# Windowed attention: strips masked by small matmuls, plain maxima, products over two or three query tiles, projections over 512 columns

## The chip, the cores and the metric

The kernel runs on one core of one Trainium2 chip. The metric is the device time of one launch in microseconds; lower is better. Engines are PE (TensorE), DVE (VectorE), ACT (ScalarE), POOL (GpSimd) and SP (the queue that issues most transfers). PSUM has eight banks of 128 x 512 fp32.

## The reference

Three layers act on x of shape (4, 2048, 256): a mixture-of-experts layer, an attention layer and the experts again. For the drawn inputs every expert is over its capacity, so that the expert layers add nothing except that their routing must be counted. The attention is what takes the time:

```
q = (x @ Wq.T).reshape(B, T, H, HD); k, v alike        # x here is layer-normed; H = 16 heads, HD = 16
attend = |i - j| <= 128  or  i == 0  or  j == 0
logits = where(attend, q @ k.T * 0.25, -inf)
out = softmax(logits) @ v;  x = x + out @ Wo.T
```

So each query looks at 257 neighbours and at key 0, and query 0 looks at all keys.

## The kernel before

A batch has 16 tiles of 128 tokens; the 16 heads go in four head groups of four. One *item* is one tile of one head group (256 items in all), one *step* handles one item in each stage, and a step has four *quarters*, one for each head. The function `schedule` writes out one global order of events, quarter by quarter, and each engine runs the events that concern it in that order. The stages lag behind one another: A at step k, B at step k - 20, the products with the values (PV) at step k - 23.

- **A (L934, L1431)**: the logits of a query tile for one head, as four strips. Strip s holds 32 queries on partitions 32s to 32s + 31, against a window of 288 keys; each strip is one bf16 matmul (q and k are stacked in bf16 pieces, 96 rows) in a column tile of its own, so that the four run side by side. The bank is one of a ring of three (`a_ring`). Then DVE adds the mask (`band`, fp32 in SBUF, one of three versions: first tile, middle, last tile) and takes the row maximum in one fused instruction (`tensor_tensor_reduce`), followed by a read of the accumulator into `row_max`. Its semaphore `a_free` gives the bank back.
- **MAX**: once per head group the maxima are turned and put as extra rows beside q.
- **B (L962, L1105)**: the logits transposed (keys on partitions), less the maxima, in a ring of two banks (`b_ring`); ACT takes the exponential into `probs`, a ring of four tiles in fp32.
- **CUT (L1218, L1223)**: POOL zeroes the two outer blocks of `probs` outside the band.
- **PV (L980)**: for query tile i, one event for each key tile j = i - 1, i, i + 1, at quarters 0, 1 and 2; each event is four fp32 matmuls (one for each head, each in its own column tile) with the 32 columns of the values as weights and 128 columns of `probs` moving. An fp32 matmul shows as two instructions. Four query tiles share the bank `o_bank`, which COPY_OUT (L1122) then copies for the division.
- **QK (L823)**: the projection of q and k for 512 tokens, fp32, as four events (two halves of 256 columns, two halves k of the contraction), each of four column tiles. ACT, DVE and POOL then cut the result in bf16 pieces and SP stacks them by DMA.
- Further fillers in the order: VALUES (L838), PROJECT (L806), transposes, norms and the work for query 0 (FIRST). `QK_AT`, `VALUES_AT` and the like give the quarter at which each starts, set by hand.

For a wait, `band_count(n)` and `pv_count(n, part)` give how many CUTs and PV events must have been done. The exponential of item n at its first head waits until PV item n - 3 has done the part with key tile n - 4, since `probs` is a ring of four. The constants are loaded by SP at the start (L668, L675).

## Time and profile before

| | us |
|---|---|
| median of 3 runs | 869.26 (867.83 to 869.36) |
| span of the profiled execution | 867.2 |
| PE busy | 814.6 (94%) |
| DVE busy | 758.3 (87%) |
| ACT busy | 637.2 (73%) |
| POOL busy | 488.1 (56%) |

The page gives the span of the profiled execution, from its first to its last instruction; its own device time beside that is not given, and the median of the timed runs lies 2.1 us above the span. How to read it: busy time is a share of the whole span, and a busy PE counts each matmul to the modelled end of its pipeline, so that small holes between matmuls don't show. PE and PEld (weight load) overlap. A distance between two starts says more on what an instruction occupies than its length, since the next one often starts before the end.

### The profile page before, as it was taken

To read this page: it belongs to the slowest core of one execution; us is meant where nothing else is said; L and a number is where in the kernel's file an instruction comes from. 1 tells how busy PE (TensorE), PEld (TensorE's weight loads), DVE (VectorE), ACT (ScalarE), POOL (GpSimd) and SP (SyncE) were. 2 spreads that over 40 slices of the span, in tenths; PEclk is the share of its full clock that TensorE was granted. 3 is DMA by queue.
4 is the path that set the end of the run, shared out by engine and by line. 5 is a ranking of instruction groups with operands and counts; after the bars stand their busy time and mean duration, and the time that the engine had idled before them with its cause. 6 is when DMAs were issued, how large, how long until landed. Compare 5 with 4: busy or idle time off the path is not lost. (4 is left out here: it accounts for less than half of the span.)

```text
span 867.2 us, 50607 instructions
## 1 busy us (share of the span) xinstructions
PE 814.6 (94%) x21504; PEld 606.9 (70%) x21505; DVE 758.3 (87%) x2819; ACT 637.2 (73%) x1417; POOL 488.1 (56%) x874
## 2 busy tenths in 40 slices
PE   9798999999999999999999999898999999999894
PEld 8555667767777777667778777666778777766572
DVE  7898899989887899998987899998988889998785
ACT  2268888897877667998877666898777766888850
POOL 3212556675555557765554465675554556656763
PEclk9999999999999999999999999999999999999998
DMA  7722224432212344441213335352222335220113
GB/s 231 116 81 75 67 73 121 135 88 70 77 62 96 111 146 119 120 127 62 89 51 101 106 105 161 108 131 71 74 73 68 106 93 149 94 77 18 49 51 102
DMA packets 93191, 83.51 MB, mean 96 GB/s; under 512 B 17568, under 2 KB 92192, under 8 KB 92960
## 3 DMA queue, kind: packets, MB, share of 16 engines
q1 hardware_dynamic: 91360, 78.91, 30.1%
q8 instruction: 171, 2.80, 1.5%
q10 hardware_dynamic: 1600, 1.31, 1.0%
q14 instruction: 60, 0.49, 0.2%
HBM read 20.66 MB, written 8.39 MB: 33 GB/s over the span
## 5 line engine op out<-in xcount | busy, mean ns | idle before, releaser
L1105 ACT ACTIVATE probs<-bank 128x384 f32<-128x384 f32 (+1 forms) x1024 | 462.8, 480 | 146.8 <-PE bank L962 137.4
L1431 DVE CUSTOM_DVE_ANT_0 bank<-bank,con 128x288 f32<-128x288 f32 x1024 | 494.4, 518 | 53.2 <-PE bank L934 44.8
L934 PE MATMUL bank<-k_stack,q_stack 96*32 96x288 bf16 x4096 | 325.4, 288 | 10.7 <-DVE row_max L1431 5.7
L962 PE MATMUL bank<-q_stack,k_stack 99*32 99x288 bf16 (+2 forms) x4096 | 319.8, 285 | 16.0 <-ACT probs L1105 9.7
L980 PE MATMUL bank<-probs,v_sb 128*32 128x128 f32 x5888 | 305.4, 272 | 3.6 <-issue 1.5
L1218 POOL TENSOR_SCALAR_AFFINE_SELECT probs<-probs 128x512 f32<-128x512 f32 x240 | 154.8, 645 | 180.1 <-ACT probs L1105 179.5
L980 PEld LDWEIGHTS bank<-probs,v_sb 128*32 128x32 f32 x5888 | 192.1, 110 | 36.7 <-issue 5.3
L962 PEld LDWEIGHTS bank<-q_stack,k_stack 99*32 99x32 bf16 x4096 | 123.6, 95 | 79.7 <-ACT probs L1105 53.5
L934 PEld LDWEIGHTS bank<-k_stack,q_stack 96*32 96x32 bf16 x4096 | 127.3, 95 | 74.0 <-DVE row_max L1431 21.3
L1223 POOL TENSOR_SCALAR_AFFINE_SELECT probs<-probs 128x512 f32<-128x512 f32 x240 | 154.1, 642 | 19.3 <-ACT probs L1105 19.2
L823 PE MATMUL bank<-xnT,wqk_sb 128*32 128x256 f32 x2048 | 158.1, 379 | 0.6 <-DVE neg_max L1453 0.5
L1431 DVE DVE_READ_ACCUMULATOR2_ANT row_max<- 128x1 f32 x1024 | 144.1, 141 | 0.0
L1206 POOL TENSOR_TENSOR pieces<-rest,pieces 128x512 bf16<-128x512 f32 x64 | 74.4, 1162 | 61.7 <-ACT pieces L1070 61.5
L838 PE MATMUL bank<-wv_sb,xnT 128*32 128x272 f32 x1024 | 83.9, 393 | 1.7 <-ACT v_sb L1077 1.1
L806 PE MATMUL bank<-wo_sb,attnT 128*32 128x264 f32 x1024 | 72.0, 386 | 1.9 <-DVE x_ring L1339 0.9
L823 PEld LDWEIGHTS bank<-xnT,wqk_sb 128*32 128x32 f32 x2048 | 64.6, 110 | 5.6 <-ACT v_sb L1077 1.2
L1055 ACT ACTIVATE pieces<-bank 128x512 bf16<-128x512 f32 x64 | 38.3, 599 | 20.7 <-PE bank L823 19.5
L1359 DVE TENSOR_TENSOR rest<-bank,pieces 128x512 f32<-128x512 f32 x64 | 44.1, 688 | 4.3 <-ACT pieces L1055 4.1
L1266 DVE BATCH_NORM_STATS2 stats<-x_ring 128x6 f32<-128x256 f32 x112 | 47.1, 421 | 0.2
L1000 PE MATMUL bank<-con,o_raw 128*32 128x68 f32 x2048 | 44.4, 223 | 2.6 <-issue 1.7
L1070 ACT ACTIVATE pieces<-rest 128x512 bf16<-128x512 f32 x64 | 40.6, 635 | 8.0 <-DVE rest L1359 7.8
L806 PEld LDWEIGHTS bank<-wo_sb,attnT 128*32 128x32 f32 x1024 | 33.2, 109 | 13.4 <-issue 2.2
(126 smaller groups left out, 737.2 us busy)
## 6 DMA issues: line engine op xcount, KB each, us to landing
q_stack<-pieces SPq DMA_DIRECT2D x384, 64.0 KB, 2.7
k_stack<-pieces SPq DMA_DIRECT2D x364, 64.0 KB, 2.7
x_ring<-in_x SPq DMA_DIRECT2D x28, 512.0 KB, 4.5
out_x<-x_ring SPq DMA_DIRECT2D x16, 512.0 KB, 3.9
attn<-in_x SPq DMA_DIRECT2D x4, 512.0 KB, 6.0
wback_sb<-in_wback SPq DMA_DIRECT2D x8, 256.0 KB, 6.0
k_stack<-pieces ACTq DMA_DIRECT2D x20, 64.0 KB, 3.6
q_stack<-neg_max SPq DMA_DIRECT2D x48, 16.0 KB, 2.3
```

What stands on the lines that cost most here:

```text
L806: last = pe.matmul(bank_of("PROJECT", i, t)[SP * s:SP * (s + 1), 0:D + E], attnT[:, t // 2, k, at:at + SP], wo_sb[:, k, :], start=(k == 0) ...
L823: last = pe.matmul(bank_of("QK", g, c)[SP * s:SP * (s + 1), 256 * half:256 * (half + 1)], wqk_sb[:, g % NG, k, SP * s:SP * (s + 1)], xnT[: ...
L838: last = pe.matmul(bank_of("VALUES", b, t)[SP * s:SP * (s + 1), 0:D + HD], xnT[:, k, at:at + SP], wv_sb[:, k, :], start=(k == 0), stop=(k ...
L934: last = pe.matmul(a_ring[i % len(a_ring)][SP * s:SP * (s + 1), 0:WIN], q_stack[g % 2][0:KROWS, h, q:q + SP], k_stack[g % 2][0:KROWS, h, q ...
L962: last = pe.matmul(b_ring[i % len(b_ring)][SP * s:SP * (s + 1), start:final], k_stack[g % 2][0:SROWS, h, WINDOW + P * j + SP * s:WINDOW + ...
L980: last = pe.matmul(o_bank[SP * h:SP * (h + 1), P * (i % 4):P * (i % 4 + 1)], v_sb[:, j, VW * head:VW * head + SP], probs[:, j % 4, h, P * ...
L1105: act.activation(probs[:, j % 4, h, c0:c1], b_ring[i % len(b_ring)][:, c0:c1], ACT.Exp, scale=LOGIT_SCALE).then_inc(S["exp_ready"], 1)
L1206: pool.tensor_tensor(pieces[i % 2][:, 2, :], rest[:, :], pieces[i % 2][:, 1, :], ALU.subtract).then_inc(S["piece3_ready"], 1)
L1218: pool.affine_select(out=part, in_=part, compare_op=ALU.is_ge, fill=0.0, base=0, pattern=[[0, HG], [1, P]], channel_multiplier=-1).then_in ...
L1223: pool.affine_select(out=part, in_=part, compare_op=ALU.is_ge, fill=0.0, base=0, pattern=[[0, HG], [-1, P]], channel_multiplier=1).then_in ...
L1266: dve.bn_stats(stats[:, t, :], x_tiles(i)[:, t, :]).then_inc(S["stats_ready"], 1)
L1431: dve.tensor_tensor_reduce(out=a_ring[i % len(a_ring)][:, 0:WIN], in0=a_ring[i % len(a_ring)][:, 0:WIN], in1=mask, scale=1.0, scalar=con[: ...
```

## The change

Three edits are made together.

1. **Mask.** The masks `band` and the identity are copied to bf16 (`band_half`, `ident_half`) by ACT at the start. After the four matmuls of an A item, PE adds the mask to the strips by matmuls with a piece of the identity as weights: for a middle tile the first 32 and the last 32 columns of the strip (64 columns, one set of four), for the first and last tile of a batch 128 columns on the open side and 32 on the other (two sets). DVE's fused instruction becomes a plain maximum over the 288 columns.
2. **Products.** A PV event is now one key tile against all the query tiles of the same bank that it serves: `products_of(i)` lists (key tile, first query tile, end), two or three tiles wide, or one where a neighbour lies in another bank. `PRODUCTS_AT` sets the quarter: (0, 1), (1), (1), (0, 2) for i mod 4. The waits on counts of PV events follow it.
3. **Projections.** A QK event takes 512 columns in place of 256, so there are two in place of four, at the first and third of the former places.

```diff
@@ -77,6 +77,8 @@
         ones = sb("ones", [P, P])
+        ident_half = sb("ident_half", [P, P], BF16)
+        band_half = sb("band_half", [P, 3, WIN], BF16)
         neg_half = sb("neg_half", [P, 4])
...
@@ -119,7 +121,7 @@
         take = ident.rearrange("p (h c) -> p h c", c=SP)[:, :, 0:VW]
-        band = [con[:, C_BAND + i * WIN:C_BAND + (i + 1) * WIN] for i in range(3)]
+        band_all = con[:, C_BAND:C_BAND + 3 * WIN].rearrange("p (i c) -> p i c", i=3)
         pick = con[:, C_PICK:C_PICK + NG * SP].rearrange("p (g c) -> p g c", g=NG)
...
@@ -361,10 +363,66 @@
+        def products_of(i):
+            parts = []
+            if i % 4 == 0 and i:
+                parts.append((i - 1, i, i + 1))
+            parts.append((i, i - (i % 4 > 0), i + 1 + (i % 4 < 3)))
+            if i % 4 == 3 and i < NT - 1:
+                parts.append((i + 1, i, i + 1))
+            return parts
+        PRODUCTS_AT = ((0, 1), (1,), (1,), (0, 2))
+        pv_before = [sum(len(products_of(t)) for t in range(i)) for i in range(NT + 1)]
         def pv_count(n, part):
             g, i = divmod(n, NT)
-            return g * (3 * NT - 2) + min(3 * i + part, 3 * NT - 2)
+            return g * pv_before[NT] + pv_before[i] + part
+        def pv_last(n):
+            j = n % NT
+            if j % 4 == 3 and j < NT - 1:
+                return pv_count(n + 1, 1)
+            return pv_count(n, 1 + (j % 4 == 0 and j > 0))
+        def mask_of(t):
+            return 0 if t == 0 else 2 if t == NT - 1 else 1
+        def both_edges(strip):
+            return strip.rearrange("p (b c) -> p b c", c=SP)[:, 0:2 * WINDOW // SP + 1:2 * WINDOW // SP, :]
+        def lower_half(strip):
+            return strip[:, 0:WINDOW]
+        def lower_edge(strip):
+            return strip[:, 0:SP]
+        def upper_half(strip):
+            return strip[:, WIN - WINDOW:WIN]
+        def upper_edge(strip):
+            return strip[:, WIN - SP:WIN]
+        def mask_parts(t):
+            if t == 0:
+                return lower_half, upper_edge
+            if t == NT - 1:
+                return lower_edge, upper_half
+            return both_edges,
...
@@ -453,8 +511,8 @@
                         apart = apart if n else OPENING["QK_APART"]
-                    for part in range(4):
-                        begin(at + apart * part, "QK", n, c, part)
+                    for k in range(KC):
+                        begin(at + 2 * apart * k, "QK", n, c, k)
                     done = at + 3 * apart + 1
...
@@ -530,10 +588,12 @@
                         events.append(("A", k, h))
-                    if 0 <= pv < items and h < 3:
-                        if 0 <= pv % NT + h - 1 < NT:
-                            events.append(("PV", pv, h))
-                        if h == 2 and pv % 4 == 3:
+                    if 0 <= pv < items:
+                        i = pv % NT
+                        for part, slot in enumerate(PRODUCTS_AT[i % 4][-len(products_of(i)):]):
+                            if slot == h:
+                                events.append(("PV", pv, part))
+                        if h == 2 and i % 4 == 3:
                             events.append(("COPY_OUT", pv // 4))
...
@@ -668,8 +728,8 @@
                         sp.dma_start(x_tiles(1), rows(dram, 1)).then_inc(S["x_first1"], 16)
+                        sp.dma_start(con[:, C_BAND:C_PICK], consts[:, C_BAND:C_PICK]).then_inc(S["band_in"], 16)
                         for dst, src in (
-                                (con[:, C_BAND:C_PICK], consts[:, C_BAND:C_PICK]),
                                 (con[:, C_DIAG:], consts[:, C_DIAG:]),
...
@@ -809,9 +869,8 @@
                         elif kind == "QK":
-                            g, c, part = n
-                            half, k = divmod(part, KC)
-                            if part == 0:
+                            g, c, k = n
+                            if k == 0:
                                 if g == 0 and first:
...
@@ -819,18 +878,17 @@
                             for s in range(4):
-                                at = 512 * c + 256 * half
-                                last = pe.matmul(bank_of("QK", g, c)[SP * s:SP * (s + 1), 256 * half:256 * (half + 1)],
+                                last = pe.matmul(bank_of("QK", g, c)[SP * s:SP * (s + 1), :],
                                                  wqk_sb[:, g % NG, k, SP * s:SP * (s + 1)],
-                                                 xnT[:, k, at:at + 256],
+                                                 xnT[:, k, 512 * c:512 * (c + 1)],
                                                  start=(k == 0), stop=(k == KC - 1))
-                            if part == 3:
+                            if k == KC - 1:
                                 last.then_inc(full_sem("QK", g, c), 1)
                         elif kind == "VALUES":
                             b, t, k = n
                             if k == 0:
                                 if first and b == 0 and t == 0:
-                                    pe.wait_ge(S["setup_in"], 16 * 5)
+                                    pe.wait_ge(S["setup_in"], 16 * 4)
                                 pe.wait_ge(*emptied("XT", early_index[b, t // 4], t % 4 // 2))
...
@@ -931,10 +990,16 @@
                                 q = P * t + SP * s
-                                last = pe.matmul(a_ring[i % len(a_ring)][SP * s:SP * (s + 1), 0:WIN],
-                                                 q_stack[g % 2][0:KROWS, h, q:q + SP],
-                                                 k_stack[g % 2][0:KROWS, h, q:q + WIN],
-                                                 start=True, stop=True)
+                                pe.matmul(a_ring[i % len(a_ring)][SP * s:SP * (s + 1), 0:WIN],
+                                          q_stack[g % 2][0:KROWS, h, q:q + SP],
+                                          k_stack[g % 2][0:KROWS, h, q:q + WIN],
+                                          start=True, stop=False)
+                            for parts in mask_parts(t):
+                                for s in range(4):
+                                    strip = a_ring[i % len(a_ring)][SP * s:SP * (s + 1), 0:WIN]
+                                    last = pe.matmul(parts(strip), ident_half[:, SP * s:SP * (s + 1)],
+                                                     parts(band_half[:, mask_of(t), :]),
+                                                     start=False, stop=parts is mask_parts(t)[-1])
                             last.then_inc(S["a_full"], 1)
...
@@ -968,20 +1033,20 @@
                             g, i = divmod(n, NT)
-                            j = i - 1 + part
-                            if g % NG == 0 and part == 2 or n % (NG * NT) == 0 and part == 1:
+                            j, first_tile, end_tile = products_of(i)[part]
+                            if g % NG == 0:
                                 pe.wait_ge(*emptied("VALUES", g // NG, j))
                             pe.wait_ge(S["band_ready"], band_count(NT * g + j))
-                            start, final = part == 0 or i == 0 and part == 1, part == 2 or j == NT - 1
-                            if start and n % 4 == 0 and n:
+                            start = i % 4 == 0 and part == 0
+                            if start and n:
                                 pe.wait_ge(S["o_copied"], n // 4)
                             for h in range(HG):
                                 head = HG * (g % NG) + h
                                 last = pe.matmul(
-                                    o_bank[SP * h:SP * (h + 1), P * (i % 4):P * (i % 4 + 1)],
+                                    o_bank[SP * h:SP * (h + 1), P * (first_tile - i // 4 * 4):P * (end_tile - i // 4 * 4)],
                                     v_sb[:, j, VW * head:VW * head + SP],
-                                    probs[:, j % 4, h, P * (i - j + 1):P * (i - j + 2)],
-                                    start=start, stop=final)
+                                    probs[:, j % 4, h, P * (first_tile - j + 1):P * (end_tile - j + 1)],
+                                    start=start, stop=True, skip_group_check=True)
                             last.then_inc(S["pv_done"], 1)
...
@@ -1007,6 +1072,10 @@
                         act.activation(warm[:, :], neg_half[:, 0:1], ACT.Identity)
+                        act.wait_ge(S["ident_in"], 16)
+                        act.activation(ident_half[:, :], ident, ACT.Copy).then_inc(S["masks_ready"], 1)
+                        act.wait_ge(S["band_in"], 16)
+                        act.activation(band_half[:, :, :], band_all, ACT.Copy).then_inc(S["masks_ready"], 1)
                         act.wait_ge(S["pads_ready"], 1)
...
@@ -1099,7 +1168,7 @@
                             if n >= 4 and h == 0:
-                                act.wait_ge(S["pv_done"], pv_count(n - 3, 0))
+                                act.wait_ge(S["pv_done"], pv_last(n - 4))
                             i = HG * n + h
...
@@ -1116,7 +1185,7 @@
                             n, = n
-                            act.wait_ge(S["pv_done"], pv_count(4 * n + 3, 2))
+                            act.wait_ge(S["pv_done"], pv_count(4 * n + 4, 0))
                             if n:
...
@@ -1420,18 +1489,12 @@
                             g, t = divmod(n, NT)
-                            mask = band[0 if t == 0 else 2 if t == NT - 1 else 1]
                             i = HG * n + h
-                            if first and n == 0 and h == 0:
-                                dve.wait_ge(S["setup_in"], 16 * 5)
                             if h == 0 and t == 0 and g >= 2:
                                 dve.wait_ge(S["p0_diff"], g - 1)
                             dve.wait_ge(S["a_full"], i + 1)
-
-                            dve.tensor_tensor_reduce(
-                                out=a_ring[i % len(a_ring)][:, 0:WIN], in0=a_ring[i % len(a_ring)][:, 0:WIN], in1=mask,
-                                scale=1.0, scalar=con[:, C_LOWEST:C_LOWEST + 1], op0=ALU.add,
-                                op1=ALU.max, accum_out=row_max[:, g % 2, h, t:t + 1]).then_inc(S["a_free"], 1)
+                            dve.tensor_reduce(row_max[:, g % 2, h, t:t + 1], a_ring[i % len(a_ring)][:, 0:WIN],
+                                              AX.X, ALU.max).then_inc(S["a_free"], 1)
                         elif kind == "MAX":
                             g, = n
                             if g:
```

## Rows read from the trace of the kernel before

**Rows 1.** The page: span, busy time of each engine, granted clock in 40 slices.

```profile
span 867.2 us, 50607 instructions
PE 814.6 (94%) x21504; PEld 606.9 (70%) x21505; DVE 758.3 (87%) x2819; ACT 637.2 (73%) x1417; POOL 488.1 (56%) x874
...
PEclk9999999999999999999999999999999999999998
```

**Rows 2.** Busy time by engine (with instruction counts), sums over three sets of stretches.

```profile
core 0: us, PE busy (x) PEld busy (x) DVE busy (x) ACT busy (x) POOL busy (x), PEclk, DMA share, GB/s
...
sum 300.00, PE 298.63 PEld 231.73 DVE 254.65 ACT 217.06 POOL 162.17; mean PE 99.55 PEld 77.24 DVE 84.88 ACT 72.35 POOL 54.06
...
sum 273.00, PE 256.18 PEld 182.65 DVE 259.84 ACT 209.61 POOL 157.10; mean PE 51.24 PEld 36.53 DVE 51.97 ACT 41.92 POOL 31.42
...
sum 200.00, PE 185.45 PEld 138.04 DVE 174.69 ACT 171.40 POOL 120.22; mean PE 37.09 PEld 27.61 DVE 34.94 ACT 34.28 POOL 24.04
```

**Rows 3.** Timeline of PE, 238 to 240 us (start, length of the merged run, instructions).

```profile
238.20 0.62 PE L823 MATMUL bank<-xnT,wqk_sb 128*32 128x256 f32 x8
238.63 0.31 PE L934 MATMUL bank<-k_stack,q_stack 96*32 96x288 bf16 x4
238.76 0.41 PE L980 MATMUL bank<-probs,v_sb 128*32 128x128 f32 x8
238.98 0.31 PE L962 MATMUL bank<-q_stack,k_stack 99*32 99x288 bf16 x4
239.10 0.62 PE L823 MATMUL bank<-xnT,wqk_sb 128*32 128x256 f32 x8
```

**Rows 4.** Waits of the whole span: total us, times, longest.

```profile
ACT probs L1105 <- PE bank L962: 137.4, 289, 1.4
...
PEld bank L962 <- ACT probs L1105: 53.5, 154, 1.7
DVE bank L1431 <- PE bank L934: 44.8, 110, 0.9
PEld bank L934 <- DVE row_max L1431: 21.3, 69, 1.0
```

**Rows 5.** Timeline of PE, 36.6 to 37.3 us.

```profile
36.64 0.28 PE L856 MATMUL bank<-xnT,wqk_sb 128*32 128x1 f32 x16
36.76 0.30 PE L934 MATMUL bank<-k_stack,q_stack 96*32 96x288 bf16 x4
```

**Rows 6.** Costliest groups, from the page.

```profile
L1105 ACT ACTIVATE probs<-bank 128x384 f32<-128x384 f32 (+1 forms) x1024 | 462.8, 480 | 146.8 <-PE bank L962 137.4
L1431 DVE CUSTOM_DVE_ANT_0 bank<-bank,con 128x288 f32<-128x288 f32 x1024 | 494.4, 518 | 53.2 <-PE bank L934 44.8
...
L1431 DVE DVE_READ_ACCUMULATOR2_ANT row_max<- 128x1 f32 x1024 | 144.1, 141 | 0.0
```

**Rows 7.** Timeline of DVE, around its two plain maxima, 47 and 58 us.

```profile
47.52 0.69 DVE L1378 TENSOR_REDUCE small<-attnT 128x1 f32<-128x512 f32 x1
48.12 0.51 DVE L1431 CUSTOM_DVE_ANT_0 bank<-bank,con 128x288 f32<-128x288 f32 x1
...
57.26 0.53 DVE L1431 CUSTOM_DVE_ANT_0 bank<-bank,con 128x288 f32<-128x288 f32 x1
57.70 0.15 DVE L1431 DVE_READ_ACCUMULATOR2_ANT row_max<- 128x1 f32 x1
57.81 0.28 DVE L1390 TENSOR_REDUCE small<-bank 1x32 f32<-1x128 f32 x1
58.07 0.52 DVE L1431 CUSTOM_DVE_ANT_0 bank<-bank,con 128x288 f32<-128x288 f32 x1
```

**Rows 8.** Opening: ACT's first work, SP's issue of the constants, and its landing.

```profile
11.90 0.60 ACT L1037 ACTIVATE xnT<-bank 128x512 f32<-128x512 f32 x1 [9.59 <-PE bank L759]
...
2.82 0.98 SPq L675 DMA_DIRECT2D con<-in_consts  x2
...
con<-in_consts SPq DMA_DIRECT2D x1, 432.0 KB, 6.2
```

**Rows 9.** Instructions of L1431: first and last start, and counts in single stretches.

```profile
L1431 DVE CUSTOM_DVE_ANT_0 bank<-bank,con x1024: 491/520/530, 26.9 to 795.6; 128x288 f32<-128x288 f32 x171
...
225.00:325.00 100.00, 62.81 (x235) 1.00 0.31 100
...
625.00:725.00 100.00, 62.46 (x233) 1.00 0.29 89
...
27.00:75.00 48.00, 40.21 (x165) 1.00 0.38 84
...
725.00:775.00 50.00, 37.13 (x149) 1.00 0.36 106
```

More of the change, by code:

```diff
@@ L925, in _ @@
                                 pe.wait_ge(S["pads_ready"], 1)
+                                pe.wait_ge(S["masks_ready"], 2)
                             if h == 0 and t in (0, 3, 7, 11):
@@ L1348, in _ @@
                             n, = n
-                            dve.wait_ge(S["pv_done"], pv_count(4 * n + 3, 2))
+                            dve.wait_ge(S["pv_done"], pv_count(4 * n + 4, 0))
                             if n:
```

2 lines of the change are left out of this document (1 added, 1 removed).

## Prediction

> **What bounds the kernel now.** I read the share of busy time first [rows 1]: PE 94%, DVE 87%, ACT 73%, at a full granted clock. That is an average, so the next view is the busy time by stretch [rows 2]. It shows three kinds of time. In three stretches of 100 us (225 to 325, 425 to 525, 625 to 725; I call them P) PE is busy 298.63 of 300 us and DVE only 85%. In five stretches that sum to 273 us (D: 27 to 75, 100 to 175, 325 to 375, 525 to 575, 725 to 775) DVE is busy 259.84 us, 95%, and PE 94%. In the remaining 200 us between 75 and 800 us (M) PE stands at 93%, DVE at 87% and ACT at 86%: nothing is full, the engines wait for one another. A busy PE can still have holes, because the end of a matmul is modelled about 0.17 us after its last column; so I look at starts. In a piece of P [rows 3] the starts follow without a hole: projection 238.20, A strips 238.63, products with the values 238.76, B strips 238.98, projection 239.10. So in P every column added to PE is paid. The waits [rows 4] say how the rest hangs together: PE's weight loads for B wait 53.5 us for the exponentials (two banks), and 21.3 us for DVE's maxima (three banks); ACT waits 137.4 us for B, so ACT is fed by PE more than it holds PE up.
>
> **Prices from starts.** Column tiles of 32 run side by side, so what counts is the distance between two sets of four. By [rows 3], 288 bf16 columns take 0.12 to 0.13 us (288/2.4 GHz is 0.120), eight instructions of 128 fp32 columns 0.22 us (two sets of 0.11, where the columns alone are 0.107), eight of 256 columns 0.43 us (two sets of 0.216; columns alone 0.213). A set thus costs its columns and 3 to 5 ns.
>
> **Mask by matmuls (L934).** Each of the 1024 A items gets a further set of four bf16 matmuls over 64 columns, 27 ns of columns; the items of the first and last tile (one in eight) get two sets, over 128 and 32 columns. No row has a bf16 set as short, so I bound it. From below the columns, 27 ns. From above by the set of one fp32 column at L856: four such sets go in 0.12 us [rows 5], so a set of almost no columns costs 30 ns, and columns and that floor in full would be 57 ns. I take 30 for the set of 64 and for that of 32, and 57 (53 of columns and 4) for that of 128: a mean of (7 x 30 + 87)/8 = 37 ns per A item. The Trainium skill, "TensorE: Matmul & The Clock Gate", section "Wait — 56ns, not 53.3ns?", gives two floors of its own, about 25 ns between starts however few the columns, and about 62 ns for each matmul where decoding is done in microcode. By the second the four extra matmuls would cost 250 ns per A item and the kernel would be over 200 us slower; the sixteen instructions in 0.12 us [rows 5] speak flatly against that here.
>
> **Products over two or three tiles (L980).** The columns stay: 46 tiles of 128 per head group before, and 2+3+3+2 per four tiles plus six singles, 46 again, after. The events go from 46 to 22 per group of 64 A items, so 48 sets fewer at 4 to 5 ns each: 0.23 us per group, 3.6 ns per A item. **Projections over 512 columns (L823)**: eight sets of 256 become four of 512, 20 ns saved per 16 A items, 1.2 ns each. Net PE price per A item: 37 - 5 = 32 ns.
>
> **The maxima (L1431).** Now a fused instruction of 518 ns and a read of the accumulator [rows 6]. What it occupies is the distance of starts: fused at 57.26, its read at 57.70 [rows 7], so 0.44 us; the read hides under the next instruction where that one waits for nothing. A plain maximum over 288 columns in PSUM has no row. The maximum over 512 columns of SBUF starts at 47.52 and the next instruction at 48.12 [rows 7]: 600 ns, which is 512/0.96 = 533 and some 70; for 288 columns that gives 370 ns. The only maximum read from PSUM takes 0.26 us from start to next start at 128 columns (57.81 to 58.07), 133 and about 120: 420 ns for 288. Against 440, a gain of 20 to 70 ns per item; I take 68, because its neighbour of equal length is the contiguous row, while the PSUM one reads with a stride and writes 32 results. The bank also comes free sooner, at about 0.46 instead of 0.58 us after the start. The Trainium skill, "VectorE: DVE Perf Modes", section "The TRN2 errata", speaks against the change: 120 cycles and the columns for a PSUM source, 425 ns here; by that figure DVE would gain 15 ns per item, and the sum below would come out 11 us higher.
>
> **Opening, waits, order.** ACT now copies the identity and the masks to bf16 before its first work, and waits for the masks' transfer, with all of ACT's queue behind it, which the turned tiles need. In the trace ACT idles 9.59 us before its first work at 11.90 us [rows 8]; the transfer is issued at 2.82 us and lands within 6.2 us, at 9.1, and 864 columns at the rate of the 0.60 us for 512 are about 1 us: done at 10.2 us. Cost nothing; if the transfer came 2 us later it would cost what it came late. PE's first A item waits for both copies at 26 us, far behind them, and no longer waits on DVE's side for other constants. Order on SP's queue is the same. The wait of an exponential for its probs buffer is moved to an earlier product or the same one: nothing.
>
> **Bursts.** The products that were 0.22 us in three of four quarters of a step become up to 0.64 us in one, and a projection event 0.86 instead of 0.43 us. With both behind one another PE spends 0.86 + 0.13 + 0.03 + 0.64 = 1.66 us between two B items, while two banks of B hold about 0.9 us of exponentials (480 ns each, [rows 6]); then the light quarters (0.16 + 0.12 us) make PE wait for ACT. In P there is a filler in nearly every quarter and ACT has 28% to spare, so nothing much; in D and M I put 0.1 us per 16 A items: 672/16 x 0.1 = 4 us (bounds 0 and 15; 15 is 0.35 us per 16 items, an exponential's wait at one such place).
>
> **The sum.** Counts of A items are half the instruction counts at L1431 [rows 9]: P 235+235+233, so 352; D 402 (165 to 149, five windows); M the rest of 1024, 270.
> P: 352 x 32 ns = +11.3 us (bounds +9, at 27 ns a set, and +18, at 57 ns), DVE's gain buys nothing.
> D: DVE would give back 402 x 68 ns = 27 us, but PE, at 94% busy before, gets 402 x 32 ns = 13 us more work; I take half of the gain, -13.5 us (bounds -25 and -3).
> M: +270 x 32 ns = 9 us of PE work, of which two thirds show, since PE waits there at times anyway: +6 us (bounds -8, where DVE's maxima are what PE waits for, and +9).
> Bursts +4. Together +11.3 - 13.5 + 6 + 4 = +7.8 us. The drain after 800 us has no A items and is left as it is. The profiled execution's span is 867.2 us; the median of the three runs is 869.26, some 2 us outside the span or from run to run, which the change leaves. So 867.2 + 7.8 + 2.1 = 877 us.
>
> **Rivals.**
> (1) DVE is the true bound outside P. For it: 95% busy in D, and PE's waits for ACT may begin with late maxima. Then D gives 25 and M 8 us, P costs 11, bursts 0 to 4: 869 - 20 = 849 to 853, or with part of it 857; I name 854. It decides where PE's holes in D are over 32 ns per A item beyond what it needs; against it PE's own 94%.
> (2) The plain maximum costs 420 ns: D then gives 3 us at most and the sum is +18: 888 us. For it the PSUM row of [rows 7].
> (3) The bursts starve ACT: +15 instead of +4, and D's gain halves again: 869 + 11 - 7 + 6 + 15 = 894 us. For it: ACT already waits 137.4 us for B [rows 4]. It decides where two bursts meet in neighbouring quarters of a stretch in which ACT is over 85% busy.
> (4) Gains and costs cancel, as they do if D gives 21 us: 869 us.
>
> **Chances.** Forecast (868 to 885 around 877) 0.42; rival 1 0.27; rival 2 0.11; rival 3 0.11; rival 4 0.09. A measurement of this kernel tells about 0.2%, 1.7 us, from no change. Faster: rival 1 and a sliver of the forecast's lower end, 0.30; same 0.10; slower 0.60. The range holds eight in ten from 857 to 892: half of rival 1 lies below, and the upper end of rival 3 above.
>
> **What would show it.** In the after trace: busy PE still full in the P stretches, with each 16 A items about 0.5 us longer (100 us for 117.5 items now, 13.6 us for 16); starts 0.03 us apart between the mask's matmuls and the next set; DVE down to about 86% in D, with starts of consecutive maxima 0.37 us apart (0.42 for rival 2); the last A item's maximum later than 795.6 us [rows 9] if I am right, earlier if rival 1 is; ACT's waits for L962 well above 137 us for rival 3. The prediction is wrong if the mask's sets cost over 60 ns, or if PE's waits for DVE's banks, 21.3 us, turn out to be only the visible part of DVE's hold on the order.

## The result, and the profile after

| | before | after |
|---|---|---|
| median of 4 runs, us | 868.96 (867.83 to 869.36) | 918.92 (917.33 to 921.3) |
| ratio to before | | 1.056, 95% interval 1.052 to 1.060 |
| span of the profiled execution | 867.2 | 919.1 |

The change costs 50 us. The forecast was 877 us with a range of 857 to 892. Of all runs behind this document one was slow, of products_only (1315 us, at a granted clock of 0.573), and it is left out of every figure. These lines of the page after answer to [rows 1, 6].

```profile
span 919.1 us, 50620 instructions
PE 855.9 (93%) x22016; PEld 551.3 (60%) x22017; DVE 680.8 (74%) x1795; ACT 630.4 (69%) x1419; POOL 488.5 (53%) x874
...
L1174 ACT ACTIVATE probs<-bank 128x384 f32<-128x384 f32 (+1 forms) x1024 | 461.3, 481 | 197.9 <-PE bank L1027 191.6
L1496 DVE TENSOR_REDUCE row_max<-bank 128x1 f32<-128x288 f32 x1024 | 429.0, 449 | 146.8 <-PE bank L1000 142.6
...
L1000 PE MATMUL bank<-band_half,ident_half 128*32 128x64 bf16 (+2 forms) x4608 | 233.5, 194 | 2.1 <-issue 2.1
```

In the kernel after, A is L993, its mask L1000, B L1027, the products L1045, the projection L881. PE got 41 us busier, DVE gave up 78 us of busy time, and the span still grew by 52. DVE now waits 142.6 us for PE (44.8 before), ACT 191.6 us (137.4 before): both are fed by PE. The waits of PE after, against [rows 4] (total us, times, longest), where it waited 53.5 us for the exponentials and 21.3 us for the maxima:

```profile
PEld bank L1027 <- ACT probs L1174: 89.1, 255, 1.9
...
PEld bank L1000 <- issue: 36.6, 112, 1.0
PEld bank L993 <- issue: 29.8, 110, 2.7
PEld bank L993 <- DVE row_max L1496: 29.6, 102, 1.1
```

The prices of the single operations came out close to those worked out from the starts. The timeline of PE after (start, length of the merged run, both in us):

```profile
382.37 0.30 PE L1027 MATMUL bank<-q_stack,k_stack 99*32 99x288 bf16 x4
382.50 0.30 PE L993 MATMUL bank<-k_stack,q_stack 96*32 96x288 bf16 x4
382.62 0.20 PE L1000 MATMUL bank<-band_half,ident_half 128*32 128x64 bf16 x4
382.65 0.29 PE L1027 MATMUL bank<-q_stack,k_stack 99*32 99x288 bf16 x4
382.78 1.03 PE L881 MATMUL bank<-xnT,wqk_sb 128*32 128x512 f32 x8
383.64 0.30 PE L993 MATMUL bank<-k_stack,q_stack 96*32 96x288 bf16 x4
```

And a line of DVE's timeline after:

```profile
130.38 1.90 DVE L1496 TENSOR_REDUCE row_max<-bank 128x1 f32<-128x288 f32 x5
```

A mask set takes 0.03 us to the next start; the projection event takes 0.86 us; five maxima in a row take 1.90 us, which with 0.45 us for the last is 0.363 us from start to start (0.438 us for the fused one with its read, the median where they follow each other).

Where the time went, I read from the starts of every 16th A item, which cut the run into 64 pieces of 16 items. P are the 24 pieces with a full PE (98% or more before: 18 to 25, 34 to 41 and 50 to 57, counted from 0). D are 23 pieces, most of them in the prediction's stretches D (0 to 4, 7 to 9, 11 to 14, 26 to 29, 42 to 45, 58 to 60), M the other 17. All in us of the profiled executions, worked out from the starts of the A matmuls in each trace:

| | to first A | P | D | M | after the last A |
|---|---|---|---|---|---|
| before | 26.4 | 328.7 | 249.5 | 189.9 | 72.7 |
| max_again (plain maxima, no mask) | 26.7 | 327.9 | 244.9 | 187.3 | 73.5 |
| products_and_projections | 26.5 | 339.6 | 264.9 | 196.6 | 74.6 |
| mask_and_max | 27.0 | 349.1 | 260.9 | 208.6 | 72.1 |
| mask_twice | 26.3 | 375.6 | 296.0 | 228.7 | 72.4 |
| after | 26.7 | 349.7 | 267.1 | 201.1 | 74.6 |

After against before: +21 in P, +18 in D, +11 in M. None of the three kinds gained. The line between D and M is a choice: with the 23 pieces outside P that have the highest busy share of DVE as D, it is +19 and +10.

A second account goes by what PE is given to do: each set of four column tiles is charged its columns at 2.4 GHz (twice for an fp32 instruction) and 4 ns, 28 ns at least, and what is left between PE's first and last matmul counts as idle. In us, an estimate from the shapes and counts in each trace:

| | charged to PE | idle of PE |
|---|---|---|
| before | 739 | 118 |
| max_again | 739 | 111 |
| products_only | 736 | 134 |
| projections_only | 738 | 137 |
| products_bunched | 739 | 150 |
| products_and_projections | 735 | 157 |
| mask_and_max | 777 | 130 |
| mask_twice | 805 | 184 |
| mask_and_products | 774 | 121 |
| after | 773 | 135 |

So the 52 us by which the span grew are 34 us of columns and sets, paid in full, and some 18 us of idle time.

### The profile page after: what moved, and what is told of

Its sections match the earlier page's. It is cut to its first block, busy times and chain, and to the rows that moved or that the text cites. A ratio compares the mean times of both kernels' runs of the same rounds, so it can differ in the third digit from the quotient of the medians.

```text
span 919.1 us, 50620 instructions
## 1 busy us (share of the span) xinstructions
PE 855.9 (93%) x22016; PEld 551.3 (60%) x22017; DVE 680.8 (74%) x1795; ACT 630.4 (69%) x1419; POOL 488.5 (53%) x874
## 4 chain that ended last, share of the span: by engine, by line
PE 76%; ACT 12%; DVE 5%; issue 4%; DMA 1%; POOL 1%; ACTq 0%; POOLq 0%; DVEq 0%
PE bank L1045 16%; PE bank L1027 14%; PE bank L881 12%; PE bank L993 10%; ACT probs L1174 7%; PE bank L896 6%; PE bank L866 5%; PE bank L1000 3%; PE bank L1065 3%; ACT pieces L1124 2%; PE bank L852 2%; PE bank L819 2%; ACT xn L1087 1%; ACT o_raw L1191 1%; ACT pieces L1139 1%
## 5 line engine op out<-in xcount | busy, mean ns | idle before, releaser
L1174 ACT ACTIVATE probs<-bank 128x384 f32<-128x384 f32 (+1 forms) x1024 | 461.3, 481 | 197.9 <-PE bank L1027 191.6
L1496 DVE TENSOR_REDUCE row_max<-bank 128x1 f32<-128x288 f32 x1024 | 429.0, 449 | 146.8 <-PE bank L1000 142.6
L1027 PE MATMUL bank<-q_stack,k_stack 99*32 99x288 bf16 (+3 forms) x4096 | 313.2, 285 | 30.5 <-ACT probs L1174 24.2
L993 PE MATMUL bank<-k_stack,q_stack 96*32 96x288 bf16 x4096 | 313.7, 288 | 6.0 <-DMA k_stack<-pieces 2.5
L1000 PE MATMUL bank<-band_half,ident_half 128*32 128x64 bf16 (+2 forms) x4608 | 233.5, 194 | 2.1 <-issue 2.1
L1045 PE MATMUL bank<-probs,v_sb 128*32 128x256 f32 (+2 forms) x2816 | 225.7, 390 | 3.5 <-ACT o_raw L1191 0.7
L1027 PEld LDWEIGHTS bank<-q_stack,k_stack 99*32 99x32 bf16 x4096 | 123.3, 95 | 126.7 <-ACT probs L1174 89.1
L1000 PEld LDWEIGHTS bank<-band_half,ident_half 128*32 128x32 bf16 x4608 | 145.2, 97 | 62.9 <-issue 36.6
L993 PEld LDWEIGHTS bank<-k_stack,q_stack 96*32 96x32 bf16 x4096 | 126.9, 96 | 85.6 <-issue 29.8
L881 PE MATMUL bank<-xnT,wqk_sb 128*32 128x512 f32 x1024 | 135.1, 596 | 0.8 <-ACT v_sb L1146 0.3
L1045 PEld LDWEIGHTS bank<-probs,v_sb 128*32 128x32 f32 x2816 | 61.3, 110 | 11.9 <-issue 6.0
L1428 DVE TENSOR_TENSOR rest<-bank,pieces 128x512 f32<-128x512 f32 x64 | 44.0, 688 | 17.7 <-ACT pieces L1124 17.6
L1304 POOL TENSOR_TENSOR glob_term<-v_all,p 128x272 f32<-128x272 f32 x64 | 41.4, 647 | 1.9 <-DVE v_all L1469 1.9
```

The lines of the kernel that those rows point to most:

```text
L881: last = pe.matmul(bank_of("QK", g, c)[SP * s:SP * (s + 1), :], wqk_sb[:, g % NG, k, SP * s:SP * (s + 1)], xnT[:, k, 512 * c:512 * (c + 1) ...
L993: pe.matmul(a_ring[i % len(a_ring)][SP * s:SP * (s + 1), 0:WIN], q_stack[g % 2][0:KROWS, h, q:q + SP], k_stack[g % 2][0:KROWS, h, q:q + WI ...
L1000: last = pe.matmul(parts(strip), ident_half[:, SP * s:SP * (s + 1)], parts(band_half[:, mask_of(t), :]), start=False, stop=parts is mask_p ...
L1027: last = pe.matmul(b_ring[i % len(b_ring)][SP * s:SP * (s + 1), start:final], k_stack[g % 2][0:SROWS, h, WINDOW + P * j + SP * s:WINDOW + ...
L1045: last = pe.matmul(o_bank[SP * h:SP * (h + 1), P * (first_tile - i // 4 * 4):P * (end_tile - i // 4 * 4)], v_sb[:, j, VW * head:VW * head ...
L1174: act.activation(probs[:, j % 4, h, c0:c1], b_ring[i % len(b_ring)][:, c0:c1], ACT.Exp, scale=LOGIT_SCALE).then_inc(S["exp_ready"], 1)
```

## The experiments

Each was timed beside the kernel before, on the same chip; its median there lay between 870.5 and 872.8 us. My theory on seeing the trace was that of columns (every column added to PE is paid, DVE's gain buys nothing); the rivals were bursts, and the prediction's own, DVE as the bound in D. A third, code (PE waiting for its own instructions), came from the second set of results.

### The three edits one by one

**mask_and_max**: the whole change without its edits to PV and QK.

```diff
 # as after, but one product event per key and query tile, and
-                    for k in range(KC):
-                        begin(at + 2 * apart * k, "QK", n, c, k)
+                    for part in range(4):
+                        begin(at + apart * part, "QK", n, c, part)
```

> The mask by matmuls with the plain maxima alone; products and projections as before. Columns theory (each column added to PE is paid in every stretch, and the time DVE gains buys nothing): the 37 ns for each of 1024 A items come out in full, 869 + 38 = 907 us. Bursts theory (the wide products and projections cause most of the 50 us of the whole change): not over 885 us. The prediction's own sum without bursts: 869 + 11 - 13 + 6 and the 5 us that the merging would have saved, 878 us.

Measured 917.47 us, ratio 1.053 (1.047 to 1.059), 10 us over the columns theory and far over the bursts theory. Mask and maxima without the merging already lose 47 us; that does not yet say that they are what the whole change loses, as the sums below show.

**products_only**: `products_of`, `PRODUCTS_AT` and their counts in the kernel before, nothing else.

> Products over two or three query tiles alone; mask and maxima fused on DVE, projections as before. Columns theory: 3.7 us of set overhead saved, 865 us. Bursts theory: 880 to 900 us, with the idle time of PE before the B strips well above before.

Measured 882.4 us, ratio 1.0135 (1.0075 to 1.0194), a loss of 12 us: the bursts theory holds, at its low end.

**projections_only**:

```diff
-                    for part in range(4):
-                        begin(at + apart * part, "QK", n, c, part)
+                    for k in range(KC):
+                        begin(at + 2 * apart * k, "QK", n, c, k)
```

> Projections of q and k over 512 columns alone. Columns theory: 1 us saved, 868 us. Bursts theory: 875 to 885 us.

Measured 888.24 us, ratio 1.020 (1.015 to 1.024), a loss of 18 us: bursts again, and dearer than I had it.

**max_only**, and the same kernel in five rounds as **max_again**:

```diff
-                            dve.tensor_tensor_reduce(
-                                out=a_ring[i % len(a_ring)][:, 0:WIN], in0=a_ring[i % len(a_ring)][:, 0:WIN], in1=mask,
-                                scale=1.0, scalar=con[:, C_LOWEST:C_LOWEST + 1], op0=ALU.add,
-                                op1=ALU.max, accum_out=row_max[:, g % 2, h, t:t + 1]).then_inc(S["a_free"], 1)
+                            dve.tensor_reduce(row_max[:, g % 2, h, t:t + 1], a_ring[i % len(a_ring)][:, 0:WIN],
+                                              AX.X, ALU.max).then_inc(S["a_free"], 1)
```

> The plain maximum in place of the fused mask and maximum, and no mask anywhere in the maxima (this part of the computation is left out, so that the maxima may be those of keys outside the band); products and projections as before. It isolates DVE's gain of 65 to 70 ns per item. If DVE bounds the stretches outside the three with a full PE, as the prediction's sum took for half of it: 869 - 13 to 869 - 30, so 839 to 856 us. Columns theory: DVE's gain buys nothing, 866 to 869 us.

> The same kernel as max_only (plain maxima, no mask in them), to settle its gain: 0.99 of the kernel before, 0.985 to 0.993, if DVE's gain is worth 8 us; 0.97 or lower was the rival that took DVE for the bound.

Measured 862.09 us, 0.990 (0.987 to 0.994), and 861.61 us, 0.991 (0.989 to 0.994). DVE's gain is worth 8 to 9 us, not nothing and not the 13 to 30 of a DVE that bounds D. In max_again DVE's busy time fell from 758.3 to 681.9 us (page) and its wait for PE rose from 44.8 to 96.6 us (waits):

```profile
PE 814.0 (95%) x21504; PEld 617.3 (72%) x21505; DVE 681.9 (79%) x1795; ACT 636.9 (74%) x1417; POOL 489.7 (57%) x874
```

```profile
DVE row_max L1485 <- PE bank L992: 96.6, 220, 1.5
PEld bank L1020 <- ACT probs L1163: 57.9, 161, 1.7
```

The three edits alone cost 47, 12 and 18 us, together 77, and the change costs 50. They don't add, so there must be something that one edit brings and another takes away.

### The mask's price, and the banks

**mask_fused**: mask_and_max with DVE's fused instruction put back.

> The mask's matmuls added, while DVE keeps the fused mask and maximum (the mask is added twice, which changes nothing in the result). It prices the matmuls with no gain on DVE. Columns theory: 869 + 38 = 907, or 917 + 8 = 925 us if DVE's gain is worth the same 8 us as without masks. If the mask's matmuls delay DVE's input in a way that the cheaper maximum then makes up for: over 930 us.

Measured 925.58 us, 1.062 (1.056 to 1.069). Against mask_and_max that is 8 us again for DVE's gain (the two intervals overlap slightly), and 55 us for the mask's matmuls, 53 ns per A item, where their columns and sets are 37. The columns theory lacks 17 us.

**max_b3** (max_only) and **after_b3** (the whole change), with

```diff
-        a_ring, b_ring, o_bank, misc = banks[0:3], banks[3:5], banks[5], banks[6:8]
+        a_ring, b_ring, o_bank, misc = banks[0:2], banks[2:5], banks[5], banks[6:8]
```

> Plain maxima without any mask in them (as in max_only: this part is left out), and the five banks shared otherwise: two for A, three for B. If PE's waits for the exponentials come from B having two banks only: below max_only's 862 us, 840 to 855, with the waits of L962's line for ACT nearly gone. If the engines' rates set the pace: 860 to 865. If A needs its third bank, since each A bank is held for PE, DVE and back: over 870 us.

> The whole change with two banks for A and three for B. Bursts theory (PE idles before B since two banks cannot bridge a wide product or projection): PE's idle time before B, 66 us now, falls to about 30 and the time from 919 to 880 to 895 us. Columns theory: PE has 771 us of columns and sets in it, so not below 890 us; 910 to 919 if the idle time merely moves to A.

Measured 879.08 us, 1.010 (1.007 to 1.013), and 941.28 us, 1.080 (1.074 to 1.085): 17 and 22 us worse. The waits moved from ACT to DVE, and grew: in max_b3 PE's weight loads wait 6.6 us for the exponentials (57.9 in max_again) and 81.1 us for the maxima (8.6):

```profile
PEld bank L992 <- DVE row_max L1485: 81.1, 181, 1.2
...
PEld bank L1020 <- ACT probs L1163: 6.6, 20, 1.2
```

A needs its third bank more than B does, even with the shorter maximum. So PE's waits for DVE's banks are large at two banks, and small at three.

### Bursts

**products_bunched**: the kernel before, its three one-tile products in quarter 0.

```diff
-                        if 0 <= pv % NT + h - 1 < NT:
-                            events.append(("PV", pv, h))
+                        for part in range(3) if h == 0 else ():
+                            if 0 <= pv % NT + part - 1 < NT:
+                                events.append(("PV", pv, part))
```

> The kernel before, with its three products of one tile each put behind one another in quarter 0, in place of one in each of quarters 0, 1 and 2: same instructions, same columns, no merging. Bursts theory: the loss of products_only (12 us) comes from bunching alone, so 878 to 885 us here. If instead the wide matmul itself costs (its waits, its order against the cut of the band): 868 to 871 us.

Measured 903.0 us, 1.038 (1.033 to 1.043): the same instructions, 32 us lost, far more than expected. Bunching needs no wide matmul to hurt. Not all of it is the starving of ACT, though: the edit also moves the last product of a step two quarters ahead, and PE's weight loads for the products then wait 12.1 us for POOL's cut, against 3.4 us before:

```profile
PEld bank L963 <- ACT probs L1106: 104.0, 279, 1.7
...
PEld bank L981 <- POOL probs L1224: 12.1, 18, 1.7
```

**projections_bunched**: the kernel before, with

```diff
-                        begin(at + apart * part, "QK", n, c, part)
+                        begin(at + 2 * apart * (part // 2), "QK", n, c, part)
```

> The kernel before, with each two of the four projection events of 256 columns put in one quarter, where the change has one event of 512: same instructions, same columns. If the loss of projections_only (17 us) is from bunching: 882 to 890 us. If it is from the wide instruction: 868 to 872 us.

Measured 888.38 us, 1.021 (1.017 to 1.025), against 888.24 for the wide projections: the wide instruction itself costs nothing that these runs can tell, its place in time is the whole loss.

**products_and_projections**: both merges, no mask.

> Wide products and wide projections with DVE's fused mask and maximum as before. If losses add: 869 + 12 + 18 = 899 us. If the rare place where both meet is what costs, more: 905 us or over. If one hides the other: 885 to 893 us.

Measured 903.57 us, 1.037 (1.034 to 1.041): the two losses add (12 + 18 = 30, measured 33). The waits show how the loss comes about. In products_only ACT waits for PE 148.0 us against 137.4 before, and PE's weight loads for B wait 106.7 us for ACT against 53.5:

```profile
ACT probs L1165 <- PE bank L1022: 148.0, 319, 1.4
PEld bank L1022 <- ACT probs L1165: 106.7, 304, 1.7
```

In products_and_projections ACT waits 173.3 us, and PE's weight loads for B wait 144.7 us:

```profile
PEld bank L1020 <- ACT probs L1163: 144.7, 388, 2.1
```

Each waits for the other in turn. The exponentials wait at most 0.7 us in all for the products that free their buffer of `probs` in any trace of this section, and not at all after, so the moved wait of the change is not the cause. A piece of the kernel after shows one turn; to the PE lines from 382.37 to 383.64 above belong these of ACT:

```profile
382.72 0.49 ACT L1174 ACTIVATE probs<-bank 128x384 f32<-128x384 f32 x1 [0.36 <-PE bank L1027]
...
383.25 0.48 ACT L1174 ACTIVATE probs<-bank 128x384 f32<-128x384 f32 x1
384.14 0.49 ACT L1174 ACTIVATE probs<-bank 128x384 f32<-128x384 f32 x1 [0.41 <-PE bank L1027]
```

B items start at 382.37 and 382.65, the projection takes PE from 382.78 to 383.64, the next B starts at 383.80. Two banks hold one exponential running and one waiting; ACT is through with both at 383.73 and idles 0.41 us. The other half of the turn, PE waiting for ACT, is in the totals (89.1 us after) and not in this piece; that it falls in the light quarters is argued, not shown.

**max_spread**: max_only with products merged two tiles wide at most, in quarters 0 and 2.

```diff
-            parts.append((i, i - (i % 4 > 0), i + 1 + (i % 4 < 3)))
+            if i % 4 in (1, 2):
+                parts += [(i, i - 1, i), (i, i, i + 2)]
+            else:
+                parts.append((i, i - (i % 4 > 0), i + 1 + (i % 4 < 3)))
...
-        PRODUCTS_AT = ((0, 1), (1,), (1,), (0, 2))
+        PRODUCTS_AT = ((0, 2), (0, 2), (0, 2), (0, 2))
```

> Plain maxima with no mask in them (left out), projections as before, and the products merged only two tiles wide at most and set in quarters 0 and 2, never three tiles in one quarter. If the loss of products_only (12 us over the kernel before) comes from 0.64 us of products in one quarter: at or under max_only's 862 us, 855 to 864. If merging itself costs: 870 to 876 us.

Measured 870.08 us, 0.997 (0.995 to 0.999), between the two expectations: 8 us worse than max_only by the medians, 5 by the ratios, where the full merging lost 12. Less bunching seems to lose less, though the two were not tried on the same kernel; one, one and one tile in quarters 0, 1 and 2 is still the best tried.

### Code

What do the mask's 17 us beyond its columns consist of? In mask_fused and mask_and_max a kind of wait grew that is small before: time in which PE waits for no semaphore ("issue"). A piece of mask_fused, weight loads:

```profile
371.39 0.17 PEld L1045 LDWEIGHTS bank<-probs,v_sb 128*32 128x32 f32 x6
373.92 0.11 PEld L1045 LDWEIGHTS bank<-probs,v_sb 128*32 128x32 f32 x1 [2.36 <-issue]
```

In the middle of a set of eight, six are done, and the seventh comes 2.36 us later, with nothing to wait for. The page counts the transfers of instructions, here called code (queue 8, 16 KB each); the line of before, that of mask_and_max, then that of mask_twice:

```profile
q8 instruction: 171, 2.80, 1.5%
```

```profile
q8 instruction: 207, 3.39, 1.6%
```

```profile
q8 instruction: 235, 3.85, 1.7%
```

The code is PE's, nearly all: mask_twice has 8192 pairs of weight load and matmul more than before and 64 transfers more, which is 128 bytes a pair, and 21504 pairs at 128 bytes are 2.75 MB of the 2.80 before. The DMA records of each trace give when these transfers end; beside them I laid the idle times of over 0.2 us of the weight loads, where the next load waits for no semaphore. Those that end 1.1 to 1.9 us after the end of a transfer are called holes here. The last column is the time in them in which no matmul ran either, an estimate from the starts of the matmuls and their columns:

| | pairs on PE | code transfers | idle times without a semaphore | of these, holes | us in holes | us without a matmul |
|---|---|---|---|---|---|---|
| products_only | 18432 | 147 | 8 | 4 | 2 | 2 |
| before | 21504 | 171 | 17 | 16 | 12 | 10 |
| after | 22016 | 175 | 127 | 24 | 12 | 7 |
| mask_and_products | 23040 | 183 | 23 | 16 | 15 | 14 |
| mask_and_projections | 25088 | 199 | 153 | 57 | 34 | 26 |
| mask_and_max | 26112 | 207 | 51 | 50 | 38 | 34 |
| mask_fused | 26112 | 207 | 54 | 52 | 44 | 41 |
| mask_twice | 29696 | 235 | 122 | 121 | 103 | 93 |

In mask_twice 121 of the 122 end in that window after a transfer, which covers 19% of the time; before, in mask_and_max and in mask_fused nearly all do. The two kernels with both the mask and wide projections have some 100 further idle times of another kind: most are about 0.3 us before the mask's weight loads, anywhere between two transfers, and in those outside the window matmuls run on (less than 1 us without a matmul in all). They cost PE nothing, and the 36.6 us of "issue" at L1000 above are mostly these. Of the 24 in the window after, matmuls ran on in 15 too.

So the holes are PE running out of instructions until the next transfer of its code has come. The three runs that follow were chosen to test that.

**mask_twice**: in mask_and_max,

```diff
-            return both_edges,
+            return both_edges, both_edges2
```

where `both_edges2` is a copy of `both_edges`.

> mask_and_max with the middle tiles' mask matmuls issued twice (the second set adds the mask again, which changes nothing). PE has 26112 pairs of weight load and matmul in mask_and_max and 29696 here, and its code 207 and some 235 transfers of 16 KB. Columns theory: 896 sets at 30 ns more, 917 + 27 = 944 us. Code theory (PE runs dry of instructions behind the transfers of its code, which it already does for some 38 us in mask_and_max against 12 before): the stalls grow more than in proportion, 960 to 1000 us.

Measured 1002.11 us, 1.149 (1.144 to 1.154): 85 us for sets whose columns and overhead are 27, even above the 960 to 1000 us of the code theory. The holes grew by 65 us, the time in them without a matmul by 59, and 59 and 27 are the 85. The largest waits of PE's weight loads, the first before the mask's:

```profile
PEld bank L1004 <- issue: 35.2, 39, 3.2
PEld bank L1031 <- ACT probs L1178: 22.1, 62, 1.2
```

**mask_and_products** and **mask_and_projections**: the whole change without its projections, and without its products.

> Mask, plain maxima and wide products, with the projections as before: 23040 pairs on PE. If effects simply add: 917 + 12 = 929 us. Code theory: the 3072 pairs fewer take away most of the 26 us of stalls that the mask brought, 895 to 910 us.

> Mask, plain maxima and projections over 512 columns, with the products as before: 25088 pairs. If effects simply add: 917 + 18 = 935 us. Code theory: a third of the stalls gone, 920 to 930 us; so clearly slower than mask_and_products.

Measured 906.31 us, 1.036 (1.033 to 1.040), and 922.88 us, 1.056 (1.053 to 1.059). Adding the wide products to the mask *gains* 11 us, where alone they lose 12; the 3072 pairs that they save take the holes from 38 to 15 us (34 to 14 without a matmul). Wide projections save 1024 pairs and cost 5 us by the medians, 3 by the ratios (the intervals overlap, so this may be nothing), where alone they cost 18; the time without a matmul in the holes fell by 8 us, so here the code theory explains a part (both have bursts, and PE's idle time from them and the mask's work can overlap, which no run separates).

## Why the prediction was wrong

Two terms of its sum failed: the bursts, put at +4 us and worth some 33 by themselves, and D, where it let DVE's shorter maximum pay for PE's new work and put -13.5 us, while the trace has +18. The time fell outside all four rivals. Rival 3 had the mechanism (ACT's waits for B rose from 137.4 to 191.6 us, its sign) with a chance of 0.11, and its 894 us is still 25 too low. By the pieces above, with 37 ns of mask for each A item, in us:

| | P | D | M | together |
|---|---|---|---|---|
| forecast, the bursts of +4 aside | +11.3 | -13.5 | +6 | +3.8 |
| measured | +21.0 | +17.6 | +11.2 | +50 |
| the mask's columns and sets | +14.2 | +13.6 | +10.1 | +38 |
| bursts, net (products_and_projections) | +10.9 | +15.4 | +6.7 | +33 |
| DVE's gain (max_again) | -0.8 | -4.6 | -2.6 | -8 |
| remainder | -3.3 | -6.8 | -3.0 | -13 |

By its steps:

**Stretches and the full PE**: right. P took all columns and gave next to nothing back for DVE. Predicted +11 there with bursts at nothing; measured +21 (24 pieces, 384 items; 32 ns each would be 12). The rest of P goes to bursts: products_and_projections alone lose 11 us in P. The step "in P there is a filler in nearly every quarter, so nothing much" was wrong.

**Prices from starts**: right for each. PE's charge rose from 739 to 773 us, 34 us, which is 1024 x 32 = 33. The plain maximum occupies 363 ns, where 370 was taken and 420 was the other end; rival 2 is out, and so is the estimate of 425 ns from the cycle table of the Trainium skill ("VectorE: DVE Perf Modes", "The TRN2 errata"), which is too dear for this operation in a run of them by 62 ns. The mask's sets follow each other at 30 ns, which leaves the Trainium skill's microcode floor ("TensorE: Matmul & The Clock Gate", "Wait — 56ns, not 53.3ns?") of 62 ns out of question, as foretold.

**D, -13.5**: failed. The term took half of DVE's 27 us as a net gain, PE's 13 us of new work already paid. Plain maxima alone gave 4.6 us in D and 8 to 9 in all, while bursts took 15 there. That DVE was busy 95% there made me take it for half a bound; with 76 us of its busy time gone in max_again, it mostly waited more for PE (96.6 us in place of 44.8).

**M, +6**: measured +11. Here too the columns were paid in full and bursts, alone 7 us, were left out.

**Bursts, +4 (0 to 15)**: the term that failed most. It is 33 us by products_and_projections, 30 by the sum of the two merges alone, twice the upper bound. The prediction did name the mechanism (rival 3, two banks that cannot bridge a wide event); its size was taken for one meeting of two bursts in 16 items, while a single projection of 0.86 us already starves ACT (0.41 us in the piece above). That the products in quarter 1 leave the others too light is my reading of the waits, and no run isolates it.

**The mask in D and M**, taken as paid out of DVE's gain in D and at two thirds in M: its 37 ns cost 53 when nothing else changed. That surplus goes with the holes of code, which the prediction does not have: 4608 more pairs of weight load and matmul in mask_fused, and 31 us more in holes without a matmul. In the change itself code plays no part that the holes would show, for the merged products take almost as many pairs away as the mask brings (22016 against 21504), and PE stood in the holes for 7 us without a matmul against 10 before. So the code helps to explain why mask and maxima without the merging lose 47 us and why the edits don't add, and not why the forecast of the change was too low. No view that I read before pointed at it, though two were there: the queue of 171 instruction transfers on the page, and the waits put down to "issue".

**Opening**: right in that it cost nothing to speak of. ACT waited 4.67 us for the masks and was done with their copy at 11.15 us, 1 us later than foretold and before its first turned tile at 11.98:

```profile
10.23 0.92 ACT L1078 ACTIVATE band_half<-con 128x864 bf16<-128x864 f32 x1 [4.67 <-DMA con<-in_consts]
```

and the first A item started at 26.7 instead of 26.4 us.

How the 50 us add up: bursts 33 (products_and_projections); on top of them the mask and the plain maxima cost 15 (903.6 to 918.9). That is 38 of columns and sets, less 8 for DVE, and a remainder of -15. I take it for work falling into idle time that the bursts had left: mask and maxima took PE's idle time from 157 to 135 us, and its waits for the exponentials from 144.7 to 89.1 us. The other way round: mask and maxima 47 (38, less 8, and 26 more of holes, the remainder of -9 being what fell into earlier waits; PE's for the exponentials fell from 53.5 to 31.2 us), the products then -11, and the projections another +13 (+17 by the ratios, since the kernel before ran at 872.8 us beside mask_and_products). The account is of charges and holes in single traces with a remainder in each order, so it proves no single part; but the sign and rough size of each rests on a run: bursts on the two bunched kernels, code on mask_twice and mask_and_products, DVE on max_again and mask_fused.

What stays open: why products bunched in quarter 0 lose 32 us and merged in quarter 1 only 12 (9 us more of waiting for POOL can be a part); how far the holes depend on data transfers at the same time (the hole of 2.36 us above fell beside a load of x of 512 KB, but no run varied that). The products' gain with the mask is read as fewer instructions, but no run removes instructions and leaves the events in their quarters. One mask matmul on the full array in place of a set of four was not tried.

**A better kernel.** max_only beats both, at 0.990 to 0.991 of before. It leaves out the mask in the maxima and nowhere else. Since the weights outside the band are cut to zero after the exponential, and a softmax is the same whatever is subtracted, a maximum over some further keys serves as well, as long as those keys' logits do not exceed the row's own by so much that the exponentials vanish. That is a condition on the inputs which a general kernel would have to guard. Where it holds, as for the inputs here, the mask that the change moved at such cost to PE was not needed there.

## What to carry to other kernels

Where two engines feed one another through two banks, keep the work between their meetings even: merging work into larger instructions saved 4 ns a set here and lost 0.4 us at a place where it left the partner without work. A spare share of an engine (ACT's 28% in P) does not show that it can wait, and a busy share (DVE's 95% in D) does not show that it is the bound; a run with that engine's work alone made shorter does. Count instructions as well as columns, and look at the code queue and at waits for "issue": with 26112 pairs in place of 21504 the mask's matmuls cost 53 ns an item where their columns and sets are 37, and an edit that removes instructions can pay for another. And ask of a masking step, before moving it, whether what it protects needs it.

## What the runs showed of the hardware

- PE consumed a transfer of code (16 KB, 128 pairs of weight load and matmul) each 5.1 us before, each 4.5 us in mask_fused and each 4.3 us in mask_twice (span by transfers). Its weight loads stood without instructions for 12, 44 and 103 us in all, and no matmul ran in 10, 41 and 93 us of that. Nearly all such holes ended 1.1 to 1.9 us after a transfer did; in mask_fused they were up to 2.4 us long. A transfer's own packets took 0.9 to 1.9 us.
- A plain maximum over 288 fp32 columns in PSUM occupies VectorE for 0.363 us; the fused add and maximum with its accumulator read 0.438 us.
- Sets of four column tiles over 64 bf16 columns follow each other in 0.03 us, and accumulate on the set before without a visible stall.
- Fp32 matmuls over 256, 384 and 512 columns in column tiles run at their columns and 2 to 3 ns: 215 to 217, 322 and 429 ns from start to start for each set of four (medians; columns alone 213, 320 and 427).
